# Gate and info convolution: nine taps on eight 32x64 tiles in place of three rows on shifted planes

## The chip, the core and the metric

One core of one Trainium2 chip runs the kernel. TensorE (PE in the rows, PEld for its weight loads) multiplies matrices into PSUM, which has eight banks of 512 float32 per partition. VectorE (DVE), ScalarE (ACT) and GpSimd (POOL) do the element work, and SyncE (SP) issues most DMAs. Each engine runs its own list of instructions in order, and semaphores order the engines among each other. The metric is the time of one execution in microseconds of the device; lower is better.

## The reference

Eight images of 32 channels and 32x32 pixels go through two blocks. The first normalizes each image row (LN1), makes q, k and v by a 1x1 and a 3x3 convolution each, applies attention over channels by head, and adds the input; then comes the part that the change is about:

```python
x = _conv(attn, o_w, 0) + x                                   # x1
xn = _ln_last(x, ln2_g, ln2_b)                                # LN2, over each row of 32 pixels
gate = gelu(_conv(_conv(xn, g1, 0), g3, 1), approximate=False)
info = _conv(_conv(xn, i1, 0), i3, 1)                         # 64 channels each
out = _conv(gate * info, r1, 0) + x                           # x2
```

The second block takes x2: a 3x3 convolution (conv1), an instance norm with leaky ReLU, a 3x3 mask convolution with sigmoid, a second 3x3 convolution (conv2), q, k and v of the masked result, and softmax attention over the 3x3 neighbours of each pixel, called the window attention in the kernel. Its result, mixed with conv2's by the mask, is added to x2.

## The kernel before

The images go in four pairs. An image row block is 8 rows of 32 pixels; partitions hold 4 row blocks x 32 channels, and the free dimension 2 images x 256 pixels. The 1x1 convolution is folded into the 3x3 weights once, on TensorE, at the start.

A 3x3 convolution on TensorE is 3 matmuls that accumulate, one for each row offset dy. For the three column offsets, the operand holds three copies of the image, each shifted by one column, on 96 partitions: the planes `sh_ln2` for gate and info, 34 rows of 32 pixels so that a border of zeros is there. They are filled from `ln2_out` by DVE (shift 0, four copies per pair), ACT (shift 2, four copies) and SP's DMAs (shift 1, four per pair), with some others for the first pair. `gate_info(pair, n)` then computes one of four parts (n // 2 is the image, n % 2 says gate or info) in one PSUM bank: 3 row offsets x 2 image halves, 512 columns each. So gate and info of an image lie in two banks, GI_BANKS, and each part has its own signal `g_i`: the GELU of image 0 starts when part 0 is done, its product with info (`gated`) when part 1 is done.

The order of the work is written out by hand. There is a prologue, in which LN1 and attention of pairs 0 and 1 and gate and info of pair 0 run; then `step(0)` and `step(1)`; then a tail for the last two pairs. `step(pair)` runs the second block of `pair`, gate and info of `pair + 1`, and attention of `pair + 2`. The order of each engine's calls in the step is the order in which it runs them. On TensorE a step goes: attn_out and qk of the later pairs, conv1, the instance norm's averages, mask_conv, conv2, window_q, window_k, scores, window_v, gate_info_all, probs_transposed, reduce_1, window_out. Between them stand fillers, `stay_busy`, bf16 matmuls whose result nobody reads. On ScalarE the second half of a step is: window_exp, v_evac, gelu 0, then (in the first step) ln1's shifted copies, gelu 1, probs_t (L720, which copies the transposed probabilities), x2's shifted copies, pv_evac. In the tail ScalarE's list begins so:

```python
gelu(last, 0)
conv1_evac(but_last)      # hc, which DVE's center() waits for
in_planes(but_last)
gelu(last, 1)
load_exp_table()
x2_planes(last)
tanh_mask(but_last)
```

and TensorE's is gate_info of the last pair in pieces between conv1, average_mean and average_var of the third pair, then mask_conv, reduce_1 and the rest. `x2_sum` on DVE adds reduce_1's result to x1; DVE and ACT then copy x2 into its shifted planes, which conv1 reads.

Of the kernel before, what the change touches and what calls it, by code (L numbers as in the profile page):

```python
# [55 lines left out]
GI_BANKS = (1, 2, 0, 3)  # L56
# [41 lines left out]
def build(nc, x, shape_consts, vectors, w1_qkv, w3_qkv, w1_gi, w3_gi, conv_w, l1_qkv, r1_t, out):  # L98
    with ExitStack() as ctx:
# [8 lines left out]
        def signal(name, per_pair, start=0):  # L108
# [15 lines left out]
        w_gi = sb("w_gi", [3 * C, 3, 2, EC])  # L124
# [15 lines left out]
        ln2_out = sb("ln2_out", [P, 2, BLK])  # L140
# [4 lines left out]
        sh_ln2 = [sb(f"sh_ln2_{n}", [3 * C, 2, PLANE]) for n in (1, 2)]  # L145
# [13 lines left out]
        gate = sb("gate", [P, 2, BANK])  # L159
        gi = sb("gi", [P, 2, BANK])  # L160
# [28 lines left out]
        s_fold, s_wready = sem("folds_in_psum"), sem("constants_prepared")  # L189
        s_busy = sem("busy_operand_set")  # L190
# [26 lines left out]
                            for e in ("dma", "dve", "act")} for i in range(2)]  # L217

        planes_by = {n: {e: signal(f"{n}_planes_{e}",
                                   [0] + [16 * (R if n == "ln2" else len(c["dma"])) for c in copies[1:]] if e == "dma"  # L220
                                   else later if n == "ln1" else 1, start=1)
                         for e in (("dma",) if n in ("ln1", "ln2") else ()) + ("dve", "act")}
                     for n in ("ln1", "ln2", "x2", "in")}
# [10 lines left out]
        g_i = signal("gate_info_in_psum", 4, start=1)  # L234
# [65 lines left out]

        def values_banks(early):

            return (1, 0) if early else (7, 4)
# [36 lines left out]
        def ln2_planes_free(engine, pair):  # L340

            if pair > 1:
                engine.wait_ge(g_i.sem, g_i.done(pair - 2))

# [8 lines left out]
        W_QKV, W_ALL = 3, 8  # L353
# [6 lines left out]
        def _(sp):  # L360
# [25 lines left out]
            def ln2_planes(pair):  # L386

                ln2_planes_free(sp, pair)
                sp.wait_ge(g_ln[1].sem, g_ln[1].done(pair))
                for r in range(R):  # L390
                    at = (1 + RH * r) * W
                    sp.dma_start(sh_ln2[pair % 2][C:2 * C, :, at:at + BLK], ln2_out[C * r:C * r + C, :, :])\
                      .then_inc(planes_by["ln2"]["dma"].sem, 16)
# [28 lines left out]
            def step(pair, norm):  # L422
# [5 lines left out]
                ln2_planes(pair + 1)  # L428
                halo(pair)
                if norm:  # L430
                    ln1_planes(pair + 3)
                else:
                    ln2_planes(pair + 2)
# [9 lines left out]
            load_res(1)  # L443
            ln1_planes(2)
# [11 lines left out]
        def _(pool):  # L456
# [100 lines left out]
            clear_edges(sh_ln2[0])  # L557
            clear_edges(sh_ln2[1])
# [29 lines left out]
        def _(act):  # L588
# [56 lines left out]
            def ln2_copies(pair, parts, done=False):  # L645

                act.wait_ge(g_ln[1].sem, g_ln[1].done(pair))
                ln2_planes_free(act, pair)
                for s, r in parts:
                    ins = shift_copies(act_copy, ln2_out, sh_ln2[pair % 2], s, (r,))  # L650
                if done:
                    ins.then_inc(planes_by["ln2"]["act"].sem, 1)
# [80 lines left out]
            def ln2_planes(pair):  # L733
                ln2_copies(pair, ([(1, R - 1)] if is_first(pair) else []) + [(2, r) for r in range(R)], done=True)

# [6 lines left out]
            def step(pair, norm):  # L742
                load_exp_table()
                if is_first(pair):
                    ln2_copies(1, [(2, r) for r in range(3)])
                else:
# [6 lines left out]
                if is_first(pair):  # L753
                    ln2_copies(1, [(2, 3)], done=True)
                else:
                    ln2_planes(pair + 1)
# [13 lines left out]
                if norm:  # L770
                    ln1_planes(pair + 3)
                    gelu(pair + 1, 1)
                else:
# [991 lines left out]
```

## Time and profile before

| | us |
|---|---|
| median of 3 runs | 212.39 (211.68 to 213.26) |
| span of the profiled execution, first to last instruction | 210.1 |
| TensorE busy | 184.5 (88%) |
| DVE busy | 161.3 (77%) |
| ACT busy | 119.4 (57%) |
| POOL busy | 70.5 (34%) |
| mean granted TensorE clock | 0.989 of full |

The runs' times include some 2 us around the span. Busy shares are means over stages that differ much; which engine sets the pace has to be read from each stage. A group of rows names the kernel's line, the engine and the operation; a float32 matmul is two matmul instructions and two weight loads. In the chain that ended last, each step is followed back to what released it.

### The profile page before, as it was taken

To read this page: it belongs to the slowest core of one execution; us is meant where nothing else is said; L and a number is where in the kernel's file an instruction comes from. 1 tells how busy PE (TensorE), PEld (TensorE's weight loads), DVE (VectorE), ACT (ScalarE), POOL (GpSimd) and SP (SyncE) were. 2 spreads that over 40 slices of the span, in tenths; PEclk is the share of its full clock that TensorE was granted. 3 is DMA by queue.
4 is the path that set the end of the run, shared out by engine and by line. 5 is a ranking of instruction groups with operands and counts; after the bars stand their busy time and mean duration, and the time that the engine had idled before them with its cause. 6 is when DMAs were issued, how large, how long until landed. Compare 5 with 4: busy or idle time off the path is not lost.

```text
span 210.1 us, 5374 instructions
## 1 busy us (share of the span) xinstructions
PE 184.5 (88%) x2158; PEld 104.0 (50%) x2167; DVE 161.3 (77%) x382; ACT 119.4 (57%) x251; POOL 70.5 (34%) x62
## 2 busy tenths in 40 slices
PE   1799879879986999899997999899799998899972
PEld 1349339333353756643576455743423345565741
DVE  6798799988768859599497986994928576992682
ACT  2175273655259461967692862775845583966850
POOL 7600803150310403660007613750044003670290
PEclk9999999978999999999999999999999999999998
DMA  6412031001501000001000040001001000000002
GB/s 199 80 57 58 2 100 50 3 0 37 163 0 50 3 5 10 3 3 39 0 3 0 3 147 13 6 3 46 4 6 47 3 0 10 8 5 8 5 2 103
DMA packets 10154, 6.75 MB, mean 32 GB/s; under 512 B 7248, under 2 KB 8496, under 8 KB 10128
## 3 DMA queue, kind: packets, MB, share of 16 engines
q1 hardware_dynamic: 9888, 5.82, 10.2%
q10 hardware_dynamic: 240, 0.58, 0.7%
q8 instruction: 17, 0.28, 0.5%
q14 instruction: 9, 0.07, 0.1%
HBM read 3.30 MB, written 1.05 MB: 21 GB/s over the span
## 4 chain that ended last, share of the span: by engine, by line
PE 53%; DVE 22%; ACT 12%; issue 5%; DMA 3%; POOL 1%; SPq 1%; DVEq 0%; ACTq 0%
PE ps L1455 20%; PE ps L1375 5%; PE ps L1368 5%; PE ps L1402 5%; PE ps L1498 4%; ACT xw L703 3%; ACT p_t L720 3%; DVE sh_in L316 3%; PE ps L1533 3%; DMA w3b<-in_w_gi 2%; ACT sh_x L608 2%; PE ps L1544 2%; DVE ln_out L968 2%; PE ps L1522 2%; PE ps L1587 2%
## 5 line engine op out<-in xcount | busy, mean ns | idle before, releaser
L1455 PE MATMUL ps<-sh_ln,w_gi 96*64 96x512 f32 x192 | 44.6, 615 | 1.7 <-DVE sh_ln L316 1.7
L473 POOL TENSOR_TENSOR ln_s<-ln_s,neg_half 128x16 f32<-128x16 f32 x7 | 20.4, 2909 | 55.5 <-DVE ln_s L947 55.5
L608 ACT ACTIVATE sh_ln<-ln_out 32x512 f32<-32x512 f32 (+2 forms) x46 | 25.6, 557 | 14.6 <-DVE ln_out L968 5.5
L1455 PEld LDWEIGHTS ps<-sh_ln,w_gi 96*64 96x64 f32 x192 | 15.4, 140 | 25.9 <-issue 25.8
L1402 PE MATMUL ps<-w_qk,sh_ln 128*128 128x128 f32 x192 | 23.2, 278 | 0.4 <-issue 0.4
L1402 PEld LDWEIGHTS ps<-w_qk,sh_ln 128*128 128x128 f32 x192 | 22.2, 192 | 1.9 <-DMA sh_ln<-ln_out 0.9
L1498 PE MATMUL ps<-sh_in,w_in 96*32 96x256 f32 x384 | 22.8, 380 | 0.0
L1368 PE MATMUL ps<-busy 128*128 128x512 bf16 x68 | 19.4, 419 | 1.3 <-issue 1.2
L608 ACT ACTIVATE sh_x<-x 32x496 f32<-32x496 f32 (+1 forms) x20 | 12.3, 616 | 9.2 <-DVE x L1093 9.0
L1498 PEld LDWEIGHTS ps<-sh_in,w_in 96*32 96x32 f32 x384 | 11.9, 109 | 10.3 <-issue 3.0
L498 POOL TENSOR_TENSOR omm<-ones,msk 128x512 f32<-128x512 f32 x4 | 7.1, 1780 | 22.6 <-DVE msk L1169 22.6
L608 ACT ACTIVATE sh_in<-act_c 32x496 f32<-32x496 f32 (+1 forms) x20 | 12.3, 616 | 2.6 <-DVE act_c L1151 2.3
L316 DVE COPY sh_in<-act_c 32x496 f32<-32x496 f32 (+1 forms) x28 | 13.2, 473 | 0.5
L1368 PEld LDWEIGHTS ps<-busy 128*128 128x128 bf16 x77 | 7.6, 107 | 11.4 <-issue 6.5
L1375 PE MATMUL ps<-sh_x,w_conv 96*32 96x512 f32 x96 | 11.1, 596 | 1.4 <-ACT sh_x L608 1.4
L505 POOL TENSOR_TENSOR res<-out,x 128x512 f32<-128x512 f32 x4 | 5.1, 1274 | 20.7 <-ACT out L671 19.1
L316 DVE COPY sh_x<-x 32x496 f32<-32x496 f32 (+1 forms) x28 | 11.5, 412 | 0.5
L1412 PE MATMUL ps<-sh_ln,w_v 128*32 128x512 f32 x96 | 11.3, 597 | 0.0
L479 POOL TENSOR_TENSOR inorm_v<-inorm_v,neg_half 128x2 f32<-128x2 f32 x4 | 4.5, 1127 | 18.1 <-DVE inorm_v L1144 18.1
L720 ACT ACTIVATE p_t<-ps 64x512 f32<-64x512 f32 x14 | 8.3, 591 | 3.8 <-PE ps L1572 3.5
L1188 DVE TENSOR_REDUCE wsm<-ps 128x8 f32<-128x480 f32 x8 | 5.2, 648 | 5.9 <-PE ps L1561 5.9
L703 ACT ACTIVATE xw<-xm 128x60 f32<-128x60 f32 x64 | 9.6, 247 | 0.0
(142 smaller groups left out, 334.6 us busy)
## 6 DMA issues: line engine op xcount, KB each, us to landing
sh_ln<-ln_out SPq DMA_DIRECT2D x27, 64.0 KB, 2.1
x_res<-in_x SPq DMA_DIRECT2D x4, 256.0 KB, 2.8
out_x<-out_s SPq DMA_DIRECT2D x4, 256.0 KB, 2.0
x_norm<-in_x SPq DMA_DIRECT2D x3, 256.0 KB, 2.9
kc<-in_shape_consts ACTq DMA_DIRECT2D x1, 450.0 KB, 4.9
w3b<-in_w_gi SPq DMA_DIRECT2D x1, 288.0 KB, 5.0
x_norm<-in_x SPq DMA_DIRECT2D x2, 128.0 KB, 2.8
xm<-xm SPq DMA_DIRECT2D x8, 25.5 KB, 1.9
```

Source lines behind the costliest of these rows:

```text
L316: ins = copy(plane(planes)[C * s:C * s + C, :, 1 + RH * r:1 + RH * r + RH, cut_left:cut_left + n], src[C * r:C * r + C, :, :].rearrange("p ...
L473: nc.gpsimd.tensor_tensor(ln_s[n][:, 3, :], ln_s[n][:, 2, :], neg_half[:, :], ALU.pow)\
L498: nc.gpsimd.tensor_tensor(omm[pair % 2][:, :], ones[:, :], msk[:, :], ALU.subtract).then_inc(g.sem, 1)
L608: return nc.scalar.activation(o, i, ACT.Copy)
L703: ins = nc.scalar.activation(xw[:, TB * ia + b, :].rearrange("p (y x) -> p y x", x=KW), xm[:, i, TH * a:TH * a + KH, TW * b:TW * b + KW], ...
L720: nc.scalar.activation(p_t[rows, 4 * R * t:4 * R * t + 4 * R, h, :], ps[rows, values_banks(early)[t], :].rearrange("p (q m) -> p q m", m=T ...
L1368: nc.tensor.matmul(ps[:, bank, at:BANK], busy[:, 0:P], busy[:, 0:BANK - at], start=True, stop=True)
L1375: mm = nc.tensor.matmul(ps[C * r:C * r + C, bank, :], weight(dy), plane(planes)[:, :, RH * r + dy:RH * r + dy + RH, 0:W], start=(dy == 0), ...
L1402: mm = nc.tensor.matmul(to, sh_ln1[pair % 2][:, d, i, WD * y:WD * y + P], w_qk[:, dy, :, :, :].rearrange("p d m c -> p (d m c)"), start=(d ...
L1412: mm = nc.tensor.matmul(ps[C * d:C * d + C, 2, :], w_v[:, dy, :], sh_ln1[pair % 2][:, d, :, WD * dy:WD * dy + WD * H], start=(dy == 0), st ...
L1455: mm = nc.tensor.matmul(ps[EC * h:EC * h + EC, GI_BANKS[n], :], w_gi[:, dy, n % 2, :], xs[:, n // 2, y:y + H // 2, 0:W], start=(dy == 0), ...
L1498: mm = nc.tensor.matmul(ps[C * r:C * r + C, bank, BLK * i:BLK * i + BLK], w_in[:, i, k, dy, :], plane(sh_in)[:, i, RH * r + dy:RH * r + dy ...
```

## The change

Gate and info are computed from one bordered copy of LN2's result, `ln2_rows`: 4 row blocks x 32 channels on partitions, 10 rows of 34 pixels for each image, of which DVE writes the inner 8x32 in LN2's last operation. The first and last of the 10 rows are the neighbouring blocks' edge rows; two DMAs per pair copy them from other partitions. The shifted planes, `ln2_out` and all copies between them are gone. The convolution is nine taps, each with its own weights for 32 input channels, in matmuls of 32 rows and 64 columns of the array: row block r takes the rows, image i the columns, and r the PSUM bank. A bank now holds gate in its first half and info in its second, and a GELU or product takes two banks' halves. One signal says that all taps are done. The first three taps (dy = 1) need no edge rows. The folded weights stand on all four row blocks, in three banks, and ScalarE copies them instead of DVE.

```diff
-GI_BANKS = (1, 2, 0, 3)
+GI_TAPS = tuple((dy, dx) for dy in (1, 0, 2) for dx in range(3))
...
-        w_gi = sb("w_gi", [3 * C, 3, 2, EC])
+        w_gi = sb("w_gi", [P, 3, 2, 3, EC])
...
-        sh_ln2 = [sb(f"sh_ln2_{n}", [3 * C, 2, PLANE]) for n in (1, 2)]
+        ln2_rows = [sb(f"ln2_rows_{n}", [P, 2, RH + 2, PW]) for n in (1, 2)]
...
-        g_i = signal("gate_info_in_psum", 4, start=1)
+        g_i = signal("gate_info_in_psum", 1, start=1)
...
+        def gate_bank(pair, r):
+
+            return r + 4 if r > 1 and is_first(pair) else r
...
+            def ln2_edges(pair):
+
+                t = ln2_rows[pair % 2]
                 sp.wait_ge(g_ln[1].sem, g_ln[1].done(pair))
...
+                sp.dma_start(t[C:P, :, 0, :], t[0:P - C, :, RH, :]).then_inc(g_edge.sem, 16)
+                sp.dma_start(t[0:P - C, :, RH + 1, :], t[C:P, :, 1, :]).then_inc(g_edge.sem, 16)
...
             def gelu(pair, i):
-                act.wait_ge(g_i.sem, g_i.at(pair, 2 * i + 1))
+                act.wait_ge(g_i.sem, g_i.done(pair))
                 act.wait_ge(g_gi.sem, g_gi.before(pair))
-                nc.scalar.activation(gate[:, i, :], ps[:, GI_BANKS[2 * i], :], ACT.Gelu).then_inc(g_gelu.sem, 1)
...
+                nc.scalar.activation(gate[:, 2 * i:2 * i + 2, :], gate_banks(pair, i)[:, :, 0:BLK], ACT.Gelu)\
+                  .then_inc(g_gelu.sem, 1)
+
+            def gate_info_taps():
+
+                act.wait_ge(s_fold, 2)
+                for s, bank in enumerate((4, 6, 7)):
+                    nc.scalar.activation(w_gi[:, s, :, :, :].rearrange("p m y o -> p (m y o)"),
+                                         ps[:, bank, 0:6 * EC], ACT.Copy).then_inc(s_gi_ready, 1)
...
                 gelu(pair + 1, 0)
                 if norm:
+                    gelu(pair + 1, 1)
                     ln1_planes(pair + 3)
+                else:
                     gelu(pair + 1, 1)
-                else:
-                    ln2_copies(pair + 2, [(2, 0)])
-                    gelu(pair + 1, 1)
...
             v4_evac(1)
             head_exp(1)
-            gelu(0, 0)
             ln1_planes(2)
             squares(1, 1)
+            gelu(0, 0)
             gelu(0, 1)
...
+                    to = ln2_rows[pair % 2][:, :, 1:1 + RH, 1:1 + W]
...
+            def gate_info_fold():
+
+                pe.wait_ge(s_w_gi, 32)
+                for s, bank in enumerate((4, 6, 7)):
+                    for m in range(2):
+                        for r in range(R):
+                            mm = nc.tensor.matmul(ps[C * r:C * r + C, bank, 3 * EC * m:3 * EC * m + 3 * EC],
+                                                  w1b[:, C * m:C * m + C], w3b[:, s, m, :], start=True, stop=True)
...
+            def gate_info(pair, taps=GI_TAPS):
+
+                xs = ln2_rows[pair % 2]
+                for dy, dx in taps:
+                    if (dy, dx) == GI_TAPS[0]:
+                        pe.wait_ge(g_ln[1].sem, g_ln[1].done(pair))
+                    elif (dy, dx) == GI_TAPS[3]:
+                        pe.wait_ge(g_edge.sem, g_edge.done(pair))
+                    for m in range(2):
+                        for i in range(2):
+                            for r in range(R):
+                                rows = slice(C * r, C * r + C)
+                                mm = nc.tensor.matmul(ps[EC * i:EC * i + EC, gate_bank(pair, r), BLK * m:BLK * m + BLK],
+                                                      w_gi[rows, dx, m, dy, :], xs[rows, i, dy:dy + RH, dx:dx + W],
+                                                      start=(m == 0 and (dy, dx) == GI_TAPS[0]),
+                                                      stop=((dy, dx) == GI_TAPS[-1]), skip_group_check=True)
+                if GI_TAPS[-1] in taps:
                     mm.then_inc(g_i.sem, 1)
...
             def reduce_1(pair):
-                pe.wait_ge(g_gi.sem, g_gi.done(pair))
                 for r in range(R):
-                    mm = nc.tensor.matmul(ps[C * r:C * r + C, 1, :], w_r1[:, r // 2, :],
-                                          gi[:, :, BLK * (r % 2):BLK * (r % 2) + BLK], start=True, stop=True)
+                    if r % 2 == 0:
+                        pe.wait_ge(g_gi.sem, g_gi.at(pair, r // 2 + 1))
+                    for i in range(2):
+                        mm = nc.tensor.matmul(ps[C * r:C * r + C, 1, BLK * i:BLK * i + BLK], w_r1[:, i, :], gi[:, r, :],
+                                              start=True, stop=True)
...
             pe.wait_ge(s_busy, 1)
-            stay_busy(12, 5)
+            stay_busy(4, 5)
+            gate_info_fold()
...
-            planes_ready("ln2", 0)
-            gate_info(0, 0)
-            pe.wait_ge(g_v4_sb.sem, g_v4_sb.done(1))
-            gate_info(0, 1)
+            pe.wait_ge(s_gi_ready, 3)
+            pe.wait_ge(s_zero, Z_PADS)
+            pe.wait_ge(g_qkt_sb.sem, g_qkt_sb.done(1))
+            gate_info(0, GI_TAPS[0:7])
             attn_out(1)
-            pe.wait_ge(g_qkt_sb.sem, g_qkt_sb.done(1))
-            gate_info(0, 2)
-            pe.wait_ge(g_x1.sem, g_x1.done(1))
-            gate_info(0, 3)
+            gate_info(0, GI_TAPS[7:9])
             stay_busy(7, 5)
             reduce_1(0)
...
             pe.wait_ge(g_x2.sem, g_x2.done(but_last))
-            gate_info(last, 0)
+            gate_info(last, GI_TAPS[0:3])
             conv1(but_last)
-            gate_info(last, 1, (0,))
+            gate_info(last, GI_TAPS[3:4])
             average_mean(but_last)
-            gate_info(last, 1, (1,))
+            gate_info(last, GI_TAPS[4:5])
             average_var(but_last)
-            gate_info(last, 1, (2,))
-            gate_info(last, 2)
-            gate_info(last, 3)
+            gate_info(last, GI_TAPS[5:9])
```

## Rows read from the trace of the kernel before

**Rows 1.** Page, part 4: chain that ended last, shares by line

```profile
PE ps L1455 20%; PE ps L1375 5%; PE ps L1368 5%; PE ps L1402 5%; PE ps L1498 4%; ACT xw L703 3%; ACT p_t L720 3%; DVE sh_in L316 3%; PE ps L1533 3%; DMA w3b<-in_w_gi 2%; ACT sh_x L608 2%; PE ps L1544 2%; DVE ln_out L968 2%; PE ps L1522 2%; PE ps L1587 2%
```

**Rows 2.** Groups by shape: count | busy us, mean ns | idle before, releaser

```profile
L1455 PEld LDWEIGHTS ps<-sh_ln,w_gi 96*64 96x64 f32 x192 | 15.4, 140 | 25.9 <-issue 25.8
...
L1085 DVE TENSOR_TENSOR gi<-ps,gate 128x512 f32<-128x512 f32 x8 | 5.5, 689 | 5.3 <-issue 4.1 <-PE ps L1455 1.1
...
L643 ACT ACTIVATE gate<-ps 128x512 f32<-128x512 f32 x8 | 4.8, 597 | 1.6 <-PE ps L1455 1.4
```

**Rows 3.** The chain in order of time: start us, length us, what

```profile
74.99 2.59 PE ps L1498 x48
...
90.18 10.30 PE ps L1455 x48
...
136.65 10.30 PE ps L1455 x48
...
153.96 2.76 PE ps L1375 x24
...
159.65 6.16 PE ps L1455 x28
```

**Rows 4.** Timeline, 95 to 105 us: start us, length us, what, [idle before]

```profile
95.57 3.18 ACT L608 ACTIVATE sh_ln<-ln_out 32x512 f32<-32x512 f32 x5 [2.18 <-DVE ln_out L980]
...
101.16 2.44 ACT L720 ACTIVATE p_t<-ps 64x512 f32<-64x512 f32 x4 [1.79 <-PE ps L1572]
...
103.66 1.10 PE L1587 MATMUL ps<-p_t,v_t 128*32 128x64 f32 x64 [0.29 <-ACT p_t L720]
```

**Rows 5.** Timeline, 157 to 169 us: instance norm, x2 of last pair

```profile
157.53 0.69 ACT L657 ACTIVATE hc<-ps,vec 128x512 f32<-128x512 f32 x1 [2.93 <-DVE st L1102]
...
158.82 0.61 DVE L1137 TENSOR_SCALAR hn<-hc,inorm_v 128x256 f32<-128x256 f32 x2
...
159.80 0.69 DVE L1151 SCALAR_TENSOR_TENSOR act_c<-hn 128x512 f32<-128x512 f32 x1
160.53 3.39 DVE L316 COPY sh_in<-act_c 32x512 f32<-32x512 f32 x7
...
168.17 0.69 DVE L1093 TENSOR_TENSOR x<-ps,x 128x512 f32<-128x512 f32 x1 [1.57 <-PE ps L1470]
```

**Rows 6.** Timeline, first 20 us: fillers, and LN1 of pair 1

```profile
12.65 2.92 PE L1368 MATMUL ps<-busy 128*128 128x512 bf16 x9 [0.22 <-issue]
...
17.55 0.69 DVE L936 SCALAR_TENSOR_TENSOR ln_c<-ln_s,x_norm 128x512 f32<-128x512 f32 x1
...
18.29 0.60 ACT L624 ACTIVATE qk_t<-ps 128x512 f32<-128x512 f32 x1 [0.90 <-PE ps L1402]
```

**Rows 7.** Timeline, 38 to 64 us: the first gate and info convolution

```profile
38.60 0.69 DVE L968 TENSOR_TENSOR ln_out<-vec,ln_d 128x512 f32<-128x512 f32 x1
...
43.33 7.07 PE L1455 MATMUL ps<-sh_ln,w_gi 96*64 96x512 f32 x24 [1.73 <-DVE sh_ln L316]
...
44.79 1.28 ACT L643 ACT_TABLE_LOAD   x1
...
50.33 1.13 PE L1438 MATMUL ps<-v,mix 128*128 128x256 f32 x4
...
53.67 0.63 ACT L596 ACTIVATE ln_q<-ln_c 128x512 f32<-128x512 f32 x1 [1.75 <-DVE ln_c L936]
...
59.44 0.69 DVE L1093 TENSOR_TENSOR x<-ps,x 128x512 f32<-128x512 f32 x1 [1.89 <-PE ps L1470]
...
63.44 2.78 PE L1375 MATMUL ps<-sh_x,w_conv 96*32 96x512 f32 x24 [1.19 <-ACT sh_x L608]
```

**Rows 8.** Page, part 6: DMA issues, count, KB each, us to landing

```profile
xm<-xm SPq DMA_DIRECT2D x8, 25.5 KB, 1.9
```

**Rows 9.** Window: length, busy PE, PEld, DVE, ACT, POOL (count); clock, DMA, GB/s

```profile
45.00:48.40 3.40, 3.40 (x10) 1.21 (x8) 3.18 (x9) 1.67 (x2) 1.98 (x1) 0.50 0.00 0
```

**Rows 10.** Timeline, step of pair 1: TensorE's wait for the halo rows

```profile
129.25 1.41 PE L1533 MATMUL ps<-xm,w_bd 128*128 128x340 f32 x4 [0.40 <-DMA xm<-xm]
```

More of the change, by code:

```diff
@@ L432, in step @@
                 else:
-                    ln2_planes(pair + 2)
+                    ln2_edges(pair + 2)
                 store(pair)
@@ L743, in step @@
                 load_exp_table()
-                if is_first(pair):
-                    ln2_copies(1, [(2, r) for r in range(3)])
-                else:
+                if not is_first(pair):
                     squares(1, pair + 1)
@@ L1004, in ln1_apply @@
             def ln1_apply(pair):
-                ln_apply(0, ln1_out, "ln1", pair)
+                ln_apply(0, pair)
                 ln1_neighbours(pair)
@@ L1243, in step @@
                 head_scores(pair + 2)
-                if is_first(pair):
-                    ln2_copies(1, [(0, 3)], done=True)
-                else:
-                    ln2_apply(pair + 1)
+                if not is_first(pair):
+                    ln_apply(1, pair + 1)
                 scaled_act(pair)
@@ L1288, in _ @@
             head_max(0)
-            ln_shift(0, ln1_out, "ln1", 1)
+            ln_shift(0, 1)
             ln1_neighbours(1)
@@ L1295, in _ @@
             ln1_center(2)
+            dve.wait_ge(s_gi_ready, 3)
             clear(ps[:, 4, :], ps[:, 7, :])
             dve.wait_ge(s_zero, Z_PADS)
-            ln_apply(1, ln2_out, "ln2", 0)
+            ln_apply(1, 0)
             head_scores(1)
-            ln2_copies(0, [(1, r) for r in range(R - 1)] + [(0, r) for r in range(R)], done=True)
             ln_var(0, 2)
@@ L1306, in _ @@
             ln2_center(1)
+            ln_var(1, 1)
             gated(0, 0)
-            ln_var(1, 1)
             gated(0, 1)
             x2_all(0)
-            ln_apply(1, ln2_out, "ln2", 1)
-            ln2_copies(1, [(0, r) for r in range(3)])
+            ln_apply(1, 1)
             step(0, True)
@@ L1357, in _ @@
             mm.then_inc(s_fold, 1)
-            pe.wait_ge(s_w_gi, 32)
-            for m in range(2):
-                for s in range(3):
-                    mm = nc.tensor.matmul(ps[C * s:C * s + C, 6, 3 * EC * m:3 * EC * m + 3 * EC],
-                                          w1b[:, C * m:C * m + C], w3b[:, s, m, :], start=True, stop=True)
-            mm.then_inc(s_fold, 1)
+            def gate_info_fold():
[5 more added lines that the diff above has]
+                                                  w1b[:, C * m:C * m + C], w3b[:, s, m, :], start=True, stop=True)
+                mm.then_inc(s_fold, 1)
             def stay_busy(n, bank, at=0):
@@ L1447, in front_read @@
                 pe.wait_ge(g_score.sem, g_score.at(pair, 3))
-            def gate_info(pair, n, rows=range(3)):
-                xs = plane(sh_ln2[pair % 2])
-                for dy in rows:
-                    for h in range(2):
-                        y = H // 2 * h + dy
-                        mm = nc.tensor.matmul(ps[EC * h:EC * h + EC, GI_BANKS[n], :], w_gi[:, dy, n % 2, :],
-                                              xs[:, n // 2, y:y + H // 2, 0:W], start=(dy == 0), stop=(dy == 2))
-                if 2 in rows:
-                    mm.then_inc(g_i.sem, 1)
@@ L1460, in gate_info_all @@
-            def gate_info_all(pair, bank_3_read_of):
-                planes_ready("ln2", pair)
-                gate_info(pair, 0)
-                pe.wait_ge(g_x1.sem, g_x1.done(bank_3_read_of))
-                for n in range(1, 4):
-                    gate_info(pair, n)
+            def gate_info(pair, taps=GI_TAPS):
[14 more added lines that the diff above has]
+                if GI_TAPS[-1] in taps:
+                    mm.then_inc(g_i.sem, 1)
@@ L1615, in step @@
                 window_v(pair)
-                gate_info_all(pair + 1, pair + 1 if norm else pair + 2)
+                if not norm:
+                    pe.wait_ge(g_x1.sem, g_x1.done(pair + 2))
+                gate_info(pair + 1)
                 probs_transposed(pair)
```

94 lines of the change are left out of this document (30 added, 64 removed).

## The prediction

> **What bounds the kernel now.** I read the chain that ended last first. Its largest line by far is the gate and info convolution, L1455, with 20% of the span [rows 1]. Then the groups by shape: L1455 has 96*64 tiles, so two column tiles work side by side, and 192 weight loads, two for each of 96 float32 matmuls [rows 2]. In order of time the chain holds one whole convolution of a pair as one piece, 10.30 us for 48 instructions [rows 3]: 0.215 us each, 0.43 us for a set of two 512-column instructions. The refine convolution L1498, whose four row blocks write 32 partitions each and so make four tiles side by side, with 256 columns, takes 2.59 us for 48 [rows 3]: 0.054 us each, so a set of four again takes 0.215 us, half the columns in half the time. TensorE's time is therefore columns per set, and more tiles in a set are free as long as they run together.
>
> The timelines tell what waits for the convolution. In the steps a GELU (0.60 us) and a product (0.69 us) of each half stand behind it [rows 2], and the first GELU of a pair runs while TensorE still computes the rest. After it ScalarE evacuates the transposed probabilities, L720, 2.44 us, and the window output L1587 starts 0.06 us behind that [rows 4]. So the stretch from the end of one gate convolution to the next conv1 is set by ScalarE's queue, not by TensorE. In the tail the order is different: the convolution of the last pair is cut into pieces around conv1 and the averages, and ends at 165.81, later than all that the mask convolution behind it needs (copies done at 163.92) [rows 3, 5].
>
> **The change, part by part.** I count in times of the kernel before, and carry the gain from stage to stage.
>
> *The convolution itself.* 9 taps x 2 outputs x 2 images x 4 row blocks are 144 matmuls, 288 instructions of 256 columns, against 48 of 512. If eight 32x64 tiles run together this is 36 sets of 0.215 = 7.74 us, 2.56 less than 10.30. Lower bound: eight together, no row shows less than 0.215 for 256 columns. Upper bound: tiles that share columns take turns, four at a time as in L1498, 72 sets = 15.5 us. I take eight, since L1455 and L1498 both run as many tiles as they name. Supply of instructions is no bound: L1587 runs 64 in 1.10 us, 0.017 each [rows 4], and 0.027 is needed.
>
> No row before shows tiles that share columns but not rows. The Trainium skill (TensorE: Matmul & The Clock Gate, Part 3) measured row and column packing together as nearly full: 16 tiles 10.6 times faster than in turn; by it the sum stays at 7.74. The same part also says that a weight load overlaps a running matmul only where the row group differs. By that rule each set would add a load, and the change would lose (a rival, below). The trace speaks against it: L1498's tiles all share rows, and its sets take the bare 0.215.
>
> *Start.* 24 fold matmuls replace 6. Three ScalarE copies of 384 columns (about 0.5 us each, an estimate from 0.60 for 512 [rows 2]) fall into ScalarE's wait before the first head softmax and cost nothing there; without that cover they would cost 1.5. The fold's 48 instructions of 192 columns, four at a time, take 12 x 0.32 = 3.8 us if all of it is at half clock. What goes is about as much: eight of the fillers L1368, at 0.32 each (9 in 2.92 [rows 6]) 2.6 us, and 12 old instructions, three at a time, 1.3 us. But the four fillers that stay now run ahead of the wait for the weights, where TensorE stood still. So qk starts sooner, its copy L624 no longer makes ScalarE wait 0.90, and the squares behind it then need only L936, done at 18.24, where L624 ended at 18.89 [rows 6]. Gain 0.6 (between 0 and 0.65).
>
> *First convolution.* TensorE has been idle for 1.73 us when it starts at 43.33, waiting for DVE's seven shifted copies; LN2's result is there at 39.29 [rows 7]. The copies go, so it starts at 41.6. The edge rows' two DMAs have the shape of the halo's, 1.9 us to landing [rows 8]; the taps that need them start 12 sets, 2.6 us, later, at 44.2, 4.9 behind LN2's result, which hides them (without this cover, some 2 us). Seven taps end at 47.6, where attn_out of pair 1 goes in. Before, the squares L596 end 3.97 after attn_out's start (50.33 to 54.30) [rows 7]; now 51.6. Only then does ScalarE reach the GELU, whose table load of 1.28 us before ran during a wait [rows 7] and now does not. 51.6 + 1.28 + 0.60 = 53.5 for the first GELU, two products 0.69 each end at 54.9, the second half of reduce_1 is four instructions of 256 columns on each tile, which in attn_out take 1.13 with start and drain [rows 7]; I take 1.05. x2 starts at 55.95, not 59.44 [rows 7]. Gain 3.5, in it the end of the stretch at half clock [rows 9].
>
> *Step of pair 0.* GELU now waits for the whole convolution, and both GELUs stand ahead of ln1's five copies, which before ran during the convolution (95.57 to 98.75). The convolution ends at 100.48 - 2.56 = 97.9 [rows 3]; two GELUs to 99.2; five copies of 3.18 to 102.4; L720, 2.44, to 104.9; window output at 104.95 instead of 103.66 [rows 4]. So 2.56 us are won on TensorE and 3.85 given back on ScalarE: 1.3 later. Queued behind: the window output, then attn_out, qk and conv1, all back to back in TensorE's order, so all of it counts. x2's five copies end at 108.1, before TensorE reaches conv1.
>
> *Step of pair 1.* Four ScalarE copies ahead of the mask's tanh go, and DVE's four ahead of the mask's product. Of that the path keeps only what window_k waited for the halo, 0.40 [rows 10], since TensorE's fillers before it stay. The second convolution ends at 146.95 - 0.40 - 2.56 = 144.0 [rows 3]; two GELUs and L720 follow, with no copies between: window output from 147.8 to 148.9.
>
> *Tail.* Three taps of 0.86, then conv1 from 151.45. The last pieces of the convolution began 5.69 behind conv1's start (153.96 to 159.65 [rows 3]); with shorter pieces between, I take 5.6, and four taps and the drain end at 151.45 + 5.6 + 3.44 + 0.2 = 160.7, where before the end was at 165.81 and the mask convolution right behind it [rows 3]. But on ScalarE the first GELU of the last pair stands ahead of conv1's copy hc, and now waits for all nine taps. hc, at 157.53 before [rows 5], starts at 161.3. Behind it: hc 0.69, centering L1137 0.61, about 0.15 for the variance, then the leaky ReLU L1151 and the copies, 4.12 (159.80 to 163.92) [rows 5]. The mask convolution starts at 166.9. Product, scaling (0.6), product, half of reduce_1: x2 at 170.0, before 168.17 [rows 5]. 1.8 later; x2's copies, conv1 of the last pair and the mask's tanh stand behind it, and all that follows.
>
> *The clock.* Three new idle stretches of TensorE: 2.3 us before reduce_1 of pair 0 (the last taps and seven fillers end near 51.9, the first product at 54.2), 3.5 us before the window output of pair 0, 6.2 us before the mask convolution in the tail. Before, 1.73 us of idle were followed by 3.4 us at 0.50, 1.2 GHz [rows 7, 9]; 1.19 us ahead of conv1 were not [rows 7]. Such a stretch costs up to 1.7 us where TensorE sets the pace. I take 0.6 for the first (slack behind it), 1.6 for the second (1.1 to 2.5), 0.95 for the third (0.5 to 1.5).
>
> *Sum.* 0.6 + 3.5 - 0.6 = 3.5 gained; 1.3 + 1.6 lost in the step of pair 0; 1.8 + 0.95 lost in the tail: 2.15 us slower. The profiled span of 210.1 becomes 212.25; with the 2.3 us between that span and the median of 212.39, **214.5 us**.
>
> **The rivals.**
> *The clock stays up* (the other side). Place: the three idle stretches. Without their 3.15 us the sum is 1.0 faster, 211.4; if the table load too falls into a wait, 1.28 less, 210.1. It decides where less than 1.0 of the 3.15 is lost. For it: 1.19 us of idle left the clock alone. Against it: 1.73 did not, and two of the stretches are longer than twice that.
> *The tiles don't run eight at once.* In turns of four each convolution takes 7.7 us more, and all four lie on the path: 214.5 + 31 = 245. For it: no row shows shared columns. Against it: every shape in the trace runs all its tiles together.
> *Each set waits for its weight loads.* L1455's loads take 0.140 [rows 2]: 36 x 0.355 = 12.8 us, 5.0 more for each convolution, 234.5. Against it: L1498. This is the rule of the Trainium skill named above.
> *The convolution's gain reaches the end.* If ScalarE's order cost nothing, it would be faster by 3 x 2.56 + 4.1 = 11.8, about 200.6. Against it: that order is written out, and in the tail hc stands behind the GELU. I give it no chance of its own.
>
> **How the numbers follow.** Forecast 0.52, own range 213 to 217 (the bounds of the half clock, and a set some 5% longer); the clock stays up in all or most places 0.33, 210 to 213.5; tiles in turns 0.12, weight loads 0.03, both over 230. The range 210.0 to 218.5 leaves out these two and a little of the others. One per cent, 2.1 us, is about what a measurement can tell. Faster by over 1%, below 210.3: a third of the clock's case, 0.12. Within 1%: the rest of it and two fifths of the forecast, 0.41. Slower, above 214.5: 0.47.
>
> **What would show it.** Right: L1455's successor in 7.7 to 7.9 us for 288 instructions; x2 of pair 0 near 56; ln1's five ScalarE copies behind two GELUs and ahead of L720; hc of the third pair behind a GELU; granted clock 0.50 after each of the three stretches. Wrong: 0.43 us a set; hc before the end of the convolution; a clock of 1.00 throughout.

## The result, and the profile of the changed kernel

The changed kernel takes 213.84 us (213.54 to 215.42) against 212.03 for the kernel before (211.05 to 213.26) beside it: a ratio of 1.0128, 95% interval 1.0085 to 1.0172. The profiled execution has a span of 211.6 us, where before had 210.1, and a mean granted clock of 0.972, where before had 0.989. Run once more later (e9 below), the changed kernel stood at 1.0216 (1.0171 to 1.0260). The ratios in this document leave out disturbed runs, among them one of 604.80 us in e9 and one of 240.56 us in e5.

The groups by shape of the kernel after (count | busy us, mean ns of one | idle before, releaser) answer to [rows 2]:

```profile
L1436 PE MATMUL ps<-ln_rows,w_gi 32*64 32x256 f32 x1152 | 33.4, 376 | 0.0
L1436 PEld LDWEIGHTS ps<-ln_rows,w_gi 32*64 32x64 f32 x1152 | 25.9, 130 | 6.0 <-issue 1.9
...
L648 ACT ACTIVATE gate<-ps 128x512 f32<-128x512 f32 x8 | 4.5, 595 | 18.6 <-PE ps L1436 18.5
```

The convolution got cheaper (33.4 us of busy TensorE, where L1455 had 44.6), and the GELUs cost what they did. But ScalarE now stands still for 18.6 us ahead of its eight GELUs, nearly all of it waiting for the convolution; before it was 1.6.

The first convolution, timeline of after, 40 to 60 us (start us, length us, what, [idle before]), answers to [rows 7]; attn_out of pair 1 is L1413:

```profile
46.99 1.13 PE L1413 MATMUL ps<-v,mix 128*128 128x256 f32 x4
...
50.97 1.28 ACT L648 ACT_TABLE_LOAD   x1
...
53.64 1.66 PE L1448 MATMUL ps<-gi,w_r 128*32 128x256 f32 x16 [2.00 <-DVE gi L1062]
...
55.36 0.69 DVE L1070 TENSOR_TENSOR x<-ps,x 128x512 f32<-128x512 f32 x1 [1.18 <-PE ps L1448]
...
59.41 1.06 PE L1350 MATMUL ps<-sh_x,w_conv 96*32 96x512 f32 x8 [1.23 <-ACT sh_x L613]
```

x2 of pair 0 comes at 55.36, 4.08 sooner than before. TensorE's 2.00 us of idle are there, but L1448 takes 1.66 us and the clock does not fall: it stands at 1.00 from there to conv1 (the last window below).

The step of pair 0, timeline of after, 84 to 109 us, answers to [rows 4]:

```profile
85.97 8.33 PE L1436 MATMUL ps<-ln_rows,w_gi 32*64 32x256 f32 x288
...
94.39 1.09 ACT L648 ACTIVATE gate<-ps 128x512 f32<-128x512 f32 x2 [5.92 <-PE ps L1436]
...
95.50 3.18 ACT L613 ACTIVATE sh_ln<-ln_out 32x512 f32<-32x512 f32 x5
...
98.71 2.44 ACT L724 ACTIVATE p_t<-ps 64x512 f32<-64x512 f32 x4
...
101.20 1.94 PE L1565 MATMUL ps<-p_t,v_t 128*32 128x64 f32 x64 [3.77 <-ACT p_t L724]
```

Two GELUs, then ln1's five copies, then the probabilities: TensorE waits 3.77 us for the last of them, and the window output L1565 then takes 1.94 us instead of 1.10. Of the 4.08 us gained 2.46 are left at its start. conv1 of the second pair starts at 107.28 (the second window below), where before, in the timeline of 95 to 120 us, it was 108.42: 1.14 are left there.

```profile
108.42 2.78 PE L1375 MATMUL ps<-sh_x,w_conv 96*32 96x512 f32 x24
```

The step of pair 1, timeline of after, 120 to 147 us, with the window queries L1500, window_k L1511 and the second whole convolution:

```profile
125.39 1.19 PE L1500 MATMUL ps<-xm,w_bd 128*128 128x128 f32 x8
...
127.28 1.31 PE L1511 MATMUL ps<-xm,w_bd 128*128 128x340 f32 x4
...
134.51 8.03 PE L1436 MATMUL ps<-ln_rows,w_gi 32*64 32x256 f32 x288
```

The window queries before, timeline of 120 to 141 us; window_k before is in [rows 10]:

```profile
126.70 1.29 PE L1522 MATMUL ps<-xm,w_bd 128*128 128x128 f32 x8
```

The tail, timeline of after, 145 to 175 us, answers to [rows 3, 5]:

```profile
149.92 2.78 PE L1350 MATMUL ps<-sh_x,w_conv 96*32 96x512 f32 x24
...
155.65 3.71 PE L1436 MATMUL ps<-ln_rows,w_gi 32*64 32x256 f32 x128
159.47 0.60 ACT L648 ACTIVATE gate<-ps 128x512 f32<-128x512 f32 x1 [9.15 <-PE ps L1436]
159.96 0.68 ACT L661 ACTIVATE hc<-ps,vec 128x512 f32<-128x512 f32 x1
...
165.56 2.79 PE L1476 MATMUL ps<-sh_in,w_in 96*32 96x256 f32 x24 [6.20 <-DVE sh_in L325]
...
169.68 0.69 DVE L1070 TENSOR_TENSOR x<-ps,x 128x512 f32<-128x512 f32 x1 [2.34 <-PE ps L1448]
```

conv1 of the third pair starts 3.97 sooner than before; its row there, timeline of 151 to 158 us:

```profile
153.89 2.78 PE L1375 MATMUL ps<-sh_x,w_conv 96*32 96x512 f32 x24
```

hc of the third pair stands behind the GELU of the last pair, which waits 9.15 us for the last pair's convolution. TensorE is done with that 6.45 sooner than before (159.36 against 165.81) and then idle for 6.20; x2 of the last pair comes 1.51 later than before, and so does the end.

The windows of the kernel after (from:to, length, busy of PE, PEld, DVE, ACT, POOL with counts, granted clock, DMA share, GB/s) show where the clock fell and where it stayed. The second runs from the window output to conv1 of the second pair, the fourth from the mask convolution to conv1 of the last pair, the fifth from reduce_1 of pair 0 to conv1:

```profile
100.65:104.06 3.41, 2.86 (x66) 2.53 (x67) 0.51 (x2) 3.34 (x6) 0.00 (x0) 0.50 0.02 5
101.20:107.28 6.08, 6.08 (x93) 5.56 (x93) 2.47 (x4) 5.62 (x9) 0.00 (x0) 0.76 0.01 3
162.09:168.92 6.83, 3.36 (x32) 1.59 (x36) 5.12 (x11) 5.16 (x8) 1.80 (x3) 0.50 0.00 0
165.56:173.68 8.12, 7.89 (x112) 4.03 (x113) 5.36 (x12) 4.99 (x9) 0.00 (x0) 0.79 0.01 2
53.64:59.41 5.77, 4.54 (x41) 3.59 (x42) 4.45 (x10) 3.22 (x6) 1.28 (x1) 1.00 0.22 82
```

### The profile page after: what moved, and what is told of

The parts are those of the page before. It is cut to its first block and busy times, and to the rows that moved or that the text cites. A ratio compares the mean times of both kernels' runs of the same rounds, so it can differ in the third digit from the quotient of the medians.

```text
span 211.6 us, 7361 instructions
## 1 busy us (share of the span) xinstructions
PE 178.3 (84%) x3178; PEld 119.6 (57%) x3187; DVE 152.8 (72%) x362; ACT 109.9 (52%) x237; POOL 70.3 (33%) x62
## 2 busy tenths in 40 slices
DMA packets 10865, 6.29 MB, mean 30 GB/s; under 512 B 8721, under 2 KB 9201, under 8 KB 10833
## 5 line engine op out<-in xcount | busy, mean ns | idle before, releaser
L1436 PE MATMUL ps<-ln_rows,w_gi 32*64 32x256 f32 x1152 | 33.4, 376 | 0.0
L1436 PEld LDWEIGHTS ps<-ln_rows,w_gi 32*64 32x64 f32 x1152 | 25.9, 130 | 6.0 <-issue 1.9
L1476 PE MATMUL ps<-sh_in,w_in 96*32 96x256 f32 x384 | 23.8, 396 | 6.2 <-DVE sh_in L325 6.2
L1377 PE MATMUL ps<-w_qk,sh_ln 128*128 128x128 f32 x192 | 23.8, 282 | 0.4 <-issue 0.4
L1377 PEld LDWEIGHTS ps<-w_qk,sh_ln 128*128 128x128 f32 x192 | 23.0, 197 | 1.8 <-DMA sh_ln<-ln_out 0.9
L613 ACT ACTIVATE sh_ln<-ln_out 32x512 f32<-32x512 f32 (+1 forms) x29 | 15.2, 524 | 9.6 <-DVE ln_out L914 4.8
L1343 PE MATMUL ps<-busy 128*128 128x512 bf16 x60 | 17.1, 413 | 1.4 <-issue 1.0
L648 ACT ACTIVATE gate<-ps 128x512 f32<-128x512 f32 x8 | 4.5, 595 | 18.6 <-PE ps L1436 18.5
L325 DVE COPY sh_x<-x 32x496 f32<-32x496 f32 (+1 forms) x28 | 11.5, 411 | 0.5
L1343 PEld LDWEIGHTS ps<-busy 128*128 128x128 bf16 x69 | 6.4, 103 | 9.0 <-issue 4.5
```

Source lines behind the costliest of these rows:

```text
L325: ins = copy(plane(planes)[C * s:C * s + C, :, 1 + RH * r:1 + RH * r + RH, cut_left:cut_left + n], src[C * r:C * r + C, :, :].rearrange("p ...
L613: return nc.scalar.activation(o, i, ACT.Copy)
L1343: nc.tensor.matmul(ps[:, bank, at:BANK], busy[:, 0:P], busy[:, 0:BANK - at], start=True, stop=True)
L1377: mm = nc.tensor.matmul(to, sh_ln1[pair % 2][:, d, i, WD * y:WD * y + P], w_qk[:, dy, :, :, :].rearrange("p d m c -> p (d m c)"), start=(d ...
L1436: mm = nc.tensor.matmul(ps[EC * i:EC * i + EC, gate_bank(pair, r), BLK * m:BLK * m + BLK], w_gi[rows, dx, m, dy, :], xs[rows, i, dy:dy + R ...
L1476: mm = nc.tensor.matmul(ps[C * r:C * r + C, bank, BLK * i:BLK * i + BLK], w_in[:, i, k, dy, :], plane(sh_in)[:, i, RH * r + dy:RH * r + dy ...
```

## The experiments

The theory: the convolution's gain is real, ScalarE's order gives it back in the step of pair 0 and in the tail, and the half clock comes from the idle that this order makes. The rivals: the clock alone, or the new convolution itself (its instructions, its weight loads).

**e1_tail_order.** In the tail hc and the in planes go ahead of the GELU. `load_gelu_table`, a dummy GELU of 128x1 into a tile of its own, is there so that a table load, if one is needed, falls into a wait; its definition and its tile are left out of this diff and those below.

```diff
-            gelu(last, 0)
             conv1_evac(but_last)
+            load_gelu_table()
             in_planes(but_last)
+            gelu(last, 0)
             gelu(last, 1)
```

> The changed kernel with ScalarE's order in the tail undone at one place: hc and ScalarE's copies of the in planes of the third pair go ahead of the last pair's first GELU; a dummy GELU of one column, put behind hc, loads the table while ScalarE waits for the leaky ReLU. Theory (the loss in the tail is ScalarE's order, the half clock follows from the idle that it makes): hc near 153.6 instead of 159.96, the in planes done near 160, TensorE's 6.2 us of idle before the mask convolution under 1 us, granted clock 1.00 there; x2 of the last pair near 163.6 instead of 169.68; 6 us faster than the changed kernel, 207 to 208.5. Rival (the clock alone is at fault, the order is hidden by the convolution that ends at 159.36 anyway): 1 to 1.5 us faster, 212.3 to 212.8. Rival (the late GELU and products of the last pair are the path, so moving them back costs as much): no change, 213 to 215.

Measured: 208.19 us (207.65 to 208.77), ratio to before 0.9791 (0.9742 to 0.9840), span 206.0. Timeline of this kernel, 150 to 165 us:

```profile
154.17 0.69 ACT L666 ACTIVATE hc<-ps,vec 128x512 f32<-128x512 f32 x1 [3.25 <-DVE st L1085]
...
160.65 1.50 PE L1482 MATMUL ps<-sh_in,w_in 96*32 96x256 f32 x24 [0.69 <-DVE sh_in L326]
...
163.99 0.69 DVE L1076 TENSOR_TENSOR x<-ps,x 128x512 f32<-128x512 f32 x1 [1.18 <-PE ps L1454]
```

hc no longer waits for the convolution, the idle is 0.69, the mask convolution has its 1.50 us back, and x2 of the last pair comes at 163.99. The span is 5.6 us shorter than that of the changed kernel, by this order and the clock that follows from it; the rivals asked for 1.5 at most.

**e2_step_order.** In the step of pair 0 ln1's copies go ahead of both GELUs.

```diff
-                gelu(pair + 1, 0)
                 if norm:
-                    gelu(pair + 1, 1)
+                    load_gelu_table()
                     ln1_planes(pair + 3)
-                else:
-                    gelu(pair + 1, 1)
+                gelu(pair + 1, 0)
+                gelu(pair + 1, 1)
```

> The changed kernel with ScalarE's order in the step of pair 0 undone: ln1's five copies go ahead of the two GELUs, behind a dummy GELU of one column that loads the table, so that they run while TensorE computes the convolution. Theory (order, and the clock as its consequence): copies from 91.4, GELUs near 94.6, window output near 98.2 instead of 101.20, TensorE's idle ahead of it under 1 us instead of 3.77, granted clock 1.00 through the window output, conv1 of the second pair near 103.0 instead of 107.28; 3 us from the order and 1.3 from the clock, 209.3 to 210. Rival (the clock alone): 1.3 us, 212.5. Rival (the copies are needed ahead of the GELU by nobody, something else is late next, as x2's planes or the halo): under 1 us, 213 to 214.

Measured: 210.04 us (209.61 to 211.02), ratio 0.9884 (0.9833 to 0.9935), span 208.1. Timeline, 82 to 110 us:

```profile
91.35 3.19 ACT L614 ACTIVATE sh_ln<-ln_out 32x512 f32<-32x512 f32 x5 [2.88 <-DVE ln_out L976]
...
95.53 2.44 ACT L729 ACTIVATE p_t<-ps 64x512 f32<-64x512 f32 x4
...
98.02 1.10 PE L1569 MATMUL ps<-p_t,v_t 128*32 128x64 f32 x64 [0.42 <-ACT p_t L729]
...
102.79 2.78 PE L1354 MATMUL ps<-sh_x,w_conv 96*32 96x512 f32 x24
```

The copies run under the convolution. The window output comes 3.18 sooner and conv1 4.49 sooner than in the changed kernel, the rest being the clock: from the window output to conv1 it is 4.77 us here, 4.76 before, 6.08 in the changed kernel. Of the 4.49 us 3.5 reach the span. The rest goes in the tail, where the order is still the changed kernel's and the half clock lasts longer in this profile: 9.24 us from the mask convolution to conv1 of the last pair, behind the same 6.20 us of idle, instead of 8.12.

```profile
161.09:170.33 9.24, 9.24 (x113) 4.74 (x117) 5.38 (x13) 5.57 (x9) 0.00 (x0) 0.65 0.01 2
```

The time lies 0.04 above the theory's range and clear of both rivals.

**e4_fillers.** The order as it is; bfloat16 matmuls of 512 columns into the two long idle stretches, so that the clock stays up.

```diff
                 reduce_1(pair + 1)
+                if norm:
+                    stay_busy(15, 6)
                 window_out(pair)
...
             gate_info(last, GI_TAPS[5:9])
+            stay_busy(26, 6)
             mask_conv(but_last, images=(0,))
```

> The changed kernel with its order as it is and 15 filler matmuls of 512 columns ahead of the window output in the step of pair 0 and 26 ahead of the mask convolution in the tail, which fill the two long idle stretches of TensorE and keep its clock up. It prices the half clock by itself. Theory (the order costs 1.6 and 4 to 5 us by itself, the half clock 1.3 in each place): 2.0 to 2.9 us faster than the changed kernel, 211 to 212, window output still near 101.2 and mask convolution near 165.6 (less 1.3 for the first), granted clock 1.00 at both. Rival (the clock is the whole loss against the forecast gain of the convolution): 6 us or more, under 208. Rival (the lost clock is hidden by slack behind it): no change, 213.5 to 214.5.

Measured: 213.88 us (211.86 to 214.81, ten runs), ratio 1.0070 (1.0031 to 1.0109), span 210.8, mean clock 0.996. Timeline:

```profile
100.67 1.10 PE L1565 MATMUL ps<-p_t,v_t 128*32 128x64 f32 x64 [0.29 <-ACT p_t L724]
...
133.12 8.69 PE L1436 MATMUL ps<-ln_rows,w_gi 32*64 32x256 f32 x288
...
164.81 1.50 PE L1476 MATMUL ps<-sh_in,w_in 96*32 96x256 f32 x24 [0.48 <-DVE sh_in L325]
...
196.07 0.41 PE L1539 MATMUL ps<-k_h,q_rows 32*32 32x60 f32 x15 [1.20 <-issue]
```

The clock gains about what was expected in each place, as the windows show:

```profile
100.67:105.43 4.76, 4.76 (x92) 4.45 (x92) 2.56 (x5) 4.67 (x7) 0.00 (x0) 1.00 0.01 3
164.81:171.78 6.97, 6.79 (x112) 5.46 (x113) 5.37 (x12) 5.01 (x9) 0.00 (x0) 1.00 0.01 2
```

The window output to conv1 takes 4.76 us instead of 6.08, and the mask convolution to conv1 of the last pair 6.97 instead of 8.12. That is 1.3 and 1.15. But the whole is some 1.2 us better by the ratios (1.0128 to 1.0070), whose intervals overlap, and 0.8 between the spans: the theory's 211 to 212 was missed, and 213.88 is the number of the rival in which the lost clock is hidden. The profile shows something else, new stalls in which TensorE waits for nothing that it shows: 1.20 us in front of the last 15 of a group of 64 instructions of L1539, and 0.66 in the second whole convolution (8.69 against 8.03). The clock is not the whole loss; whether a part of it is hidden could not be told from this run.

**e8_fillers_f32 and e9_after_again.** The same stretches filled by 10 float32 matmuls with half the added instructions; and the changed kernel itself, unedited, beside it.

```diff
+            def stay_busy_f32(n, bank):
+                for _ in range(n):
+                    nc.tensor.matmul(ps[:, bank, :], kc[:, 0:P], kc[:, 0:BANK], start=True, stop=True)
...
                 if norm:
+                    stay_busy_f32(4, 6)
...
+            stay_busy_f32(6, 6)
             mask_conv(but_last, images=(0,))
```

> The changed kernel, its two long idle stretches of TensorE filled with float32 fillers, 4 ahead of the window output in the step of pair 0 and 6 ahead of the mask convolution in the tail, in place of 15 and 26 bfloat16 ones: the same filled time with some 40 more instructions instead of 81. In the run with bfloat16 fillers the clock stayed at 1.00 and the two places each gained over 1 us, but TensorE then stood still without a wait that the profile shows, 0.66 us inside the second whole convolution and 1.20 us near 196. Theory (the half clock costs 1.2 to 1.4 us in each place, and the fillers' own instructions brought the new stalls): 211.0 to 212.0, no stall over 0.5 us of that kind behind the first convolution. Rival (the lost clock has slack behind it, whatever fills the idle): 213.2 to 214.2. Rival (the stalls come with any shift of the instructions): a stall of 0.6 to 1.3 us again, at another place, and 212.5 to 214.

> The changed kernel once more, on the same chip as the run with float32 fillers, so that the two can be compared directly: 213.0 to 214.7 by every theory.

Measured: the fillers 212.85 us (211.88 to 214.74, ten runs), ratio 1.0056 (1.0017 to 1.0095); the changed kernel 216.04 to 216.76 in three runs, ratio 1.0216 (1.0171 to 1.0260), outside what every theory expected. So filling the idle was worth some 3.5 us here. Windows of the changed kernel here, from the window output to conv1 and from the mask convolution to conv1 of the last pair:

```profile
101.81:109.51 7.70, 7.70 (x92) 7.05 (x93) 3.73 (x7) 5.85 (x9) 0.00 (x0) 0.60 0.01 2
167.86:176.47 8.61, 8.61 (x112) 4.36 (x113) 5.37 (x12) 4.99 (x9) 0.00 (x0) 0.71 0.01 2
```

The program is the same and the idle ahead nearly so, 3.60 and 6.20 us where the first profile had 3.77 and 6.20, but the half clock lasts longer: 7.70 against 4.76 at full clock costs 2.94, where the first profile had 1.32; 8.61 against 6.97 costs 1.64, where it had 1.15. What the half clock costs is thus not fixed by the kernel. Nor is it all that made this run slower: of the 2.8 us between the spans of the two profiles 0.88 is there already at attn_out of pair 1 (47.87 against 46.99). In the profile of the float32 fillers it fell in a place where the changed kernel had kept it, behind the same 2.00 us of idle ahead of reduce_1 of pair 0:

```profile
55.22 2.35 PE L1453 MATMUL ps<-gi,w_r 128*32 128x256 f32 x16 [2.00 <-DVE gi L1062]
...
198.12 1.48 PE L1481 MATMUL ps<-sh_in,w_in 96*32 96x256 f32 x18 [0.50 <-issue]
```

reduce_1 to conv1 is 6.45 there against 5.77: 0.68 lost. An unexplained stall is there again, shorter (0.50) and elsewhere. So the theory's 211 to 212 was not met, though against the changed kernel beside it the gain is more than the 1.8 to 2.8 us that this range means against 213.84. The number is that of the rival in which stalls come with any shift of the instructions, but the stall is under the 0.6 to 1.3 us that it asked for; the profiled execution does not prove that cause. With either kind of filler the changed kernel stays 0.6 to 0.7% slower than before: without the order's correction the clock does not make it a gain.

**e5_before_late_gelu.** The old convolution with the new wait.

```diff
             def gelu(pair, i):
-                act.wait_ge(g_i.sem, g_i.at(pair, 2 * i + 1))
+                act.wait_ge(g_i.sem, g_i.done(pair))
```

> The kernel before, with its old convolution, and only one wait changed: each GELU waits for all four parts of the convolution of its pair, as in the changed kernel, instead of its own part. Theory (the order costs what it costs whatever the convolution): window output of pair 0 near 107.4 instead of 103.66, hc of the third pair near 166.5 instead of 157.53, mask convolution there near 173; some 12 to 14 us slower than before, 223 to 227. Rival (what the changed kernel loses comes from its tiles, their weight loads or their 288 instructions): within 2 us of before, 212 to 214.

Measured: 235.14 us (233.81 to 235.56, three runs), ratio 1.1044 (1.0974 to 1.1113), 23 us slower: the direction of the theory, nearly twice its size. Timeline:

```profile
57.06 2.55 ACT L608 ACTIVATE sh_ln<-ln_out 32x512 f32<-32x512 f32 x4
...
61.87 1.94 PE L1470 MATMUL ps<-gi,w_r 128*32 128x512 f32 x8 [3.86 <-DVE gi L1085]
...
112.55 1.93 PE L1587 MATMUL ps<-p_t,v_t 128*32 128x64 f32 x64 [0.54 <-ACT p_t L720]
...
163.67 1.93 PE L1587 MATMUL ps<-p_t,v_t 128*32 128x64 f32 x64 [2.57 <-ACT p_t L720]
...
187.03 2.79 PE L1498 MATMUL ps<-sh_in,w_in 96*32 96x256 f32 x24 [6.14 <-DVE sh_in L316]
```

The expectation counted two places. There are four. In the prologue four copies stand between the two GELUs, and conv1 of pair 0 is 5.2 us late (68.64 against 63.44, the half clock among it); the step of pair 0 adds 3.7 at the window output, as expected, and 1.5 of half clock behind it; the step of pair 1 adds 3.1 at its window output, by four copies of LN2's planes that the changed kernel no longer has, and 1.5 of clock; the tail adds 6.2 ahead of the mask convolution and 1.9 behind it. 5.2 + 5.2 + 4.6 + 8.1 = 23.1. None of it has anything to do with the tiles.

**e6_table_early.** The dummy GELU behind the second head softmax in the prologue.

```diff
             head_exp(1)
+            load_gelu_table()
             ln1_planes(2)
```

> The changed kernel with one dummy GELU of one column behind the second head softmax's exponential in the prologue, so that the GELU table is loaded while ScalarE waits and not between the first convolution's end and the first GELU, where the trace has 1.28 us of table load. Theory (the first GELU is on the path through x2 of the first pair): x2 of pair 0 near 54.1 instead of 55.36, TensorE's idle ahead of reduce_1 0.7 instead of 2.00, and what follows sooner by as much: 1.0 to 1.3 us faster than the changed kernel, 212.5 to 212.9. Rival (behind x2 something else is late, as the planes of LN1 or the weights): x2 sooner but conv1 of pair 0 at the same time, no change, 213.5 to 214.2.

Measured: 213.43 us (213.21 to 213.87), ratio 1.0120 (1.0058 to 1.0182): a difference to the changed kernel's 1.0128 that is too small to tell from nothing. Timeline, 40 to 62 us:

```profile
47.63 1.13 PE L1419 MATMUL ps<-v,mix 128*128 128x256 f32 x4
...
54.90 0.69 DVE L1076 TENSOR_TENSOR x<-ps,x 128x512 f32<-128x512 f32 x1 [1.18 <-PE ps L1454]
...
59.25 2.78 PE L1356 MATMUL ps<-sh_x,w_conv 96*32 96x512 f32 x24 [1.54 <-ACT sh_x L614]
```

In the profile the prologue stands 0.64 later than in the changed kernel's (attn_out of pair 1 at 47.63 against 46.99), and x2 of pair 0 comes at 54.90. From attn_out to x2 it is 7.27 instead of 8.37, 1.1 us of the 1.3 expected; from attn_out to conv1 11.62 instead of 12.42, so that 0.8 remain. The step is right in kind, but the time, above the theory's 212.5 to 212.9, does not show it: the later start takes 0.64, and the half clock, again longer in the tail (8.61 from the mask convolution to conv1 instead of 8.12), takes more than the rest, so that the span is 212.0.

**e7_all_orders.** The edits of e1, e2 and e6 together.

```diff
             head_exp(1)
+            load_gelu_table()
...
+                if norm:
+                    load_gelu_table()
+                    ln1_planes(pair + 3)
                 gelu(pair + 1, 0)
-                if norm:
-                    gelu(pair + 1, 1)
-                    ln1_planes(pair + 3)
-                else:
-                    gelu(pair + 1, 1)
+                gelu(pair + 1, 1)
...
+            conv1_evac(but_last)
+            load_gelu_table()
+            in_planes(but_last)
             gelu(last, 0)
-            conv1_evac(but_last)
-            in_planes(but_last)
             gelu(last, 1)
```

> The three edits of ScalarE's order together: hc and the in planes ahead of the last pair's GELU in the tail, ln1's copies ahead of both GELUs in the step of pair 0, and the table loaded early in the prologue. Theory (the three losses lie one behind the other on the path, so they add): 5.6 + 3.8 + 1.2 = 10.6 us faster than the changed kernel, 202.5 to 204.5, no granted clock of 0.50 between 20 us and the end's last microsecond, faster than the kernel before by 8 to 9 us. Rival (one gain uses up the slack that another needs): 205 to 207.

Measured: 202.44 us (201.99 to 202.78) against 211.38 beside it, ratio 0.9602 (0.9532 to 0.9672): 4% faster than the kernel before. A window of this kernel over nearly its whole span:

```profile
30.00:199.00 169.00, 153.57 (x3001) 104.66 (x3001) 127.88 (x288) 94.58 (x208) 58.69 (x40) 1.00 0.08 22
```

and its timeline, the mask convolution of the tail:

```profile
154.77 1.50 PE L1482 MATMUL ps<-sh_in,w_in 96*32 96x256 f32 x24 [0.69 <-DVE sh_in L326]
```

The clock is 1.00 from 30 to 199 us. The span is 200.1, 11.5 shorter than the changed kernel's, while the spans of e1, e2 and e6 alone were 5.6 and 3.5 shorter and 0.4 longer. Taken from stage to stage the gains do add: from conv1 of the third pair to conv1 of the last e1 took 17.47 us (150.53 to 168.00) instead of 23.76 (149.92 to 173.68), 6.29 less; from conv1 of pair 0 to conv1 of the second pair e2 took 43.62 (59.17 to 102.79) instead of 47.87 (59.41 to 107.28), 4.25 less; e6 gained 0.80 from attn_out to conv1; together 11.34. In the single edits a part was lost again at the place that was left unmended, where the half clock happened to last longer: 9.24 instead of 8.12 in the tail of e2, and 7.25 instead of 6.08 in the step of pair 0 of e1, where the window is:

```profile
100.62:107.87 7.25, 7.25 (x93) 6.60 (x93) 3.28 (x6) 5.88 (x9) 0.00 (x0) 0.64 0.01 2
```

## Why the prediction came out as it did

It said 214.5; it is 213.84, in the main for the reasons given. That it came so close is in part luck: the terms below miss by 0.3 to 0.6 us each, some one way and some the other, and the same program took 216.31 us in e9, because the half clock lasted longer there and the start was later.

*The convolution.* 0.215 us a set was forecast. The second whole convolution takes 8.03 us, of which the last instruction is 0.38: (8.03 - 0.38) / 35 = 0.219. So eight tiles run together, and the rivals "in turns" and "weight loads" are out. With these 288 instructions go as many weight loads, in tiles that share rows. The rule of the Trainium skill (TensorE: Matmul & The Clock Gate, Part 3), that a weight load overlaps a running matmul only where the row group differs, is not borne out here; its packing of rows and columns is.

*Start and first convolution.* Forecast 0.6 and 3.5, with 0.6 of half clock lost behind x2: x2 of pair 0 was to be 4.1 sooner and is 4.08; the table load stands where it was put. At the start ScalarE's copy of qk comes 0.79 sooner than in [rows 6], but its wait for TensorE, which was to vanish, is still 0.84 (timeline of after, 0 to 30 us):

```profile
17.50 0.60 ACT L629 ACTIVATE qk_t<-ps 128x512 f32<-128x512 f32 x1 [0.84 <-PE ps L1377]
```

The half clock ahead of conv1 did not come in this execution. That is the step that failed, by 0.6, and most of the 0.65 by which the sum was too slow (2.15 forecast, 1.5 between the spans). It was not wrong in kind, as the profile of e8 shows with 0.68.

*Step of pair 0.* 1.3 was to be given back by ScalarE's order, 1.62 was, 0.3 of it a pause within the convolution (8.33 against 8.03); 1.6 by the half clock, 1.3 was. e2 shows order and clock to be the cause. For the pause the prediction had no term, having called the supply of instructions no bound; what makes it stays open.

*Step of pair 1.* The gain at window_k was forecast as its wait for the halo, 0.40. It is 0.83 (from 1.14 to 1.97, 129.25 before and 127.28 after), and that wait is gone. The term was mis-sized: 0.17 more is there already at the window queries (126.70 before, 125.39 after), which the forecast took to be held by TensorE's own fillers, and the rest comes between them and window_k.

*Tail.* The forecast put hc at 161.3, behind the GELU, in times that leave out the gains made earlier. What can be compared is the loss from conv1 of the third pair to x2 of the last. Forecast were 2.44 (153.89 to 151.45) + 1.8, and half to all of 0.95 for the clock, together 4.7 to 5.2; measured 3.97 + 1.51 = 5.48, of which the clock is 1.15 (8.12 against 6.97). e1 shows that the order is the cause.

*The clock stays up.* Kept up by fillers, the kernel is 0.6 to 0.7% slower than before, not 0.5% faster as that rival had it. In e4 its two terms were about right (1.3 and 1.15 against 1.6 and 0.95), but in the same profile stalls of 1.20 and 0.66 us stand against them.

*The gain reaches the end.* The prediction gave it no chance as the order stood, and it did not come. e7 shows that most of it does with the order changed: 10.0 us between the spans of before and e7, where 11.8 was the bound.

## What to carry to other kernels

When a piece of work that was done in parts is done in one stream, every consumer that waited for a part now waits for the whole: list what stands behind that wait in the consumer's queue, above all work for another stage. Here two places of ScalarE's order were worth 9 us of span and the sign of the change. Fillers that keep the clock up treat the symptom; the order that makes the idle is the thing to mend.

## What the runs showed of the hardware beyond that

- The same idle does not always bring the same clock. Behind 2.00 us of idle the clock stayed at 1.00 in the changed kernel and fell in e8; behind 3.77 and 3.60 us in two executions of the changed kernel the half clock cost 1.32 and 2.94 us. Behind 6.20 us of idle ahead of the mask convolution it cost 1.15 us in the changed kernel, 1.64 in e9 and 2.27 in e2 (8.12, 8.61 and 9.24 against 6.97).
- TensorE stands still at times for 0.3 to 1.2 us without a wait that the profile shows, within a group of equal instructions and at other places when instructions are added. The changed kernel has 7361 instructions, before 5374, and the page counts 25 packets on the instruction queue, before 17. That instructions came late would fit, but it was not tested and stays open.
